# An attention stage whose engines follow one timetable, with a quarter of VectorE's subtractions given to GpSimd

## What is computed

```
Q, K, V = x1 projected by Wq, Wk, Wv (256 x 256), 16 heads of 16 channels, 512 positions, 8 batches
att = (Q K^T) / 4 + b;  att = att * m + (1 - m) * -1e30     # m: a mask value per key
y   = softmax(att) V
scores = y router_w;  the 2 best of 8 experts with normalized weights
out = x1 + sum over experts e of weight_e * down_e(silu(gate_e(y)) * up_e(y))
```

## Time and profile before

| | us |
|---|---|
| median of the runs | 3030.24 |
| profiled execution, its own time | 3030.47 |
| its span, first to last instruction | 3028.6 |
| TensorE busy | 2534.4 (84%) |
| VectorE busy | 2531.1 (84%) |
| ScalarE busy | 1214.7 (40%) |
| GpSimd busy | 1348.8 (45%) |

### The profile page before, as it was taken

The page is one execution under the profiler, slowest core; times in us unless marked ns, Lnnn a source line. Parts: engine busy times, 40 slices in busy tenths (PEclk is TensorE's granted clock), DMA queues, the critical chain, the costliest instruction groups (busy, mean ns, idle before and its releaser), DMA issues. The chain is left out here.

```text
span 3028.6 us, 112026 instructions
## 1 busy us (share of the span) xinstructions
PE 2534.4 (84%) x41104; PEld 1773.0 (59%) x41104; DVE 2531.1 (84%) x11914; ACT 1214.7 (40%) x4102; POOL 1348.8 (45%) x3951
## 2 busy tenths in 40 slices
PE   4478888888888888888888778888888876999999
PEld 4356666666666666666666546666666652444444
DVE  7989999999999999999998459999999976445544
ACT  3343333333333333333333348888888850000000
POOL 6846566656565656655655224434343344000000
PEclk6599999999999999999999889999999998999999
DMA  4100000000000000000000341111111110000000
GB/s 183 43 20 3 10 10 10 10 3 10 10 10 3 10 10 10 10 3 10 10 10 3 129 136 47 32 30 47 47 47 47 33 71 0 15 13 28 0 28 14
DMA packets 43893, 88.57 MB, mean 29 GB/s; under 512 B 7168, under 2 KB 23808, under 8 KB 41600
## 3 DMA queue, kind: packets, MB, share of 16 engines
q1 hardware_dynamic: 36336, 63.11, 6.6%
q10 hardware_dynamic: 4752, 10.49, 0.9%
q0 software_dynamic: 2304, 8.39, 0.9%
HBM read 65.18 MB, written 16.78 MB: 27 GB/s over the span
## 5 line engine op out<-in xcount | busy, mean ns | idle before, releaser
L228 PE MATMUL rest<-Tl,CW 128*128 128x56 f16 x16384 | 618.9, 190 | 313.5 <-DVE Tl L494 313.5
L228 PEld LDWEIGHTS rest<-Tl,CW 128*128 128x128 f16 x16384 | 503.3, 97 | 560.5 <-DVE Tl L494 556.6
L347 ACT ACTIVATE Tf<-X 128x32 f32<-128x32 f32 x768 | 176.0, 229 | 778.5 <-DVE X L538 778.5
L1082 ACT ACTIVATE Pr<-negL,nM 128x512 f32<-128x512 f32 x512 | 357.9, 729 | 16.8 <-DVE nM L1112 16.8
L1112 DVE CUSTOM_DVE_ANT_0 negL<-Lps,negC 128x512 f32<-128x512 f32 x512 | 339.6, 682 | 21.2 <-PE Lps L1020 18.0
L1030 PE MATMUL Tps<-idS,Pr 128*128 128x128 f32 x2048 | 282.9, 282 | 87.2 <-ACT Pr L1082 86.9
L1132 DVE TENSOR_TENSOR PT<-Tps,PT 128x512 f16<-128x512 f32 x512 | 348.2, 681 | 7.3 <-ACT PT L1089 2.5
L625 POOL TENSOR_TENSOR G<-X,Dr 128x32 f32<-128x32 f32 x768 | 205.9, 268 | 301.7 <-DVE X L499 274.2
L1089 ACT ACTIVATE PT<-Tps 128x512 f16<-128x512 f32 x512 | 292.3, 597 | 98.1 <-PE Tps L1030 98.0
L1030 PEld LDWEIGHTS Tps<-idS,Pr 128*128 128x128 f32 x2048 | 222.0, 142 | 177.5 <-ACT Pr L1082 148.3
L217 PE MATMUL main<-Th,CW 128*128 128x56 f16 x8224 | 264.1, 189 | 10.2 <-DVE CW L450 10.2
(11 more groups left out here) (133 smaller groups left out, 5147.1 us busy)
## 6 DMA issues: line engine op xcount, KB each, us to landing
stage<-w_up SPq DMA_DIRECT2D x8, 1024.0 KB, 4.8
qk<-qkp ACTq DMA_DIRECT2D x32, 256.0 KB, 2.4
QR<-qk SPq DMA_DIRECT2D x128, 64.0 KB, 2.2
KR<-qk SPq DMA_DIRECT2D x128, 64.0 KB, 2.4
wstage<-moe_up POOLq DMA_DIRECT2D x16, 512.0 KB, 5.4
W2m<-w_down SPq DMA_DIRECT2D x1, 4096.0 KB, 13.4
stage<-x_tb SPq DMA_DIRECT2D x16, 256.0 KB, 2.7
x<-stage SPq DMA_DIRECT2D x16, 256.0 KB, 2.1
```

The costliest lines, as they stand in the source:

```text
L228: last = pe.matmul(rest[:, m], CW[:, 0, k, m * P:(m + 1) * P], Tl[:, k:k + 1, :].to_broadcast([P, REP, B]), start=(m == 0 and k == 0), sto ...
L1082: act.activation(Pr[:, h % 2, qt, :], negL[:, qt, :], ACT.Exp, bias=nM[:, h % 4, qt:qt + 1], scale=-1.0).then_inc(s_exp, 1)
```

## The change

**Heads in one line.** The index `j` runs over all 128 heads, and every engine has a new order within a step. **Tile 3** (`KD` = 3, the last key tile) is no longer split by ScalarE and VectorE: ScalarE copies it in f32 to `last_f`, and GpSimd casts and subtracts it (`split_last`). **The products with V** are made in halves, queries 0 and 1 at the end of one step, 2 and 3 early in the next. **`negC` has two buffers**, so the mask terms of the next batch, their sum included, are made in head 12. The `halt` instructions behind most waits of this part are gone.

```diff
@@ GpSimd, heads
+            def split_last(b, h):
+                i = b * NH + h
+                pool.wait_ge(s_cp, i + 1 + AHEAD)
+                pool.tensor_copy(PT[:, h % 2, 0, KD, :], last_f[:, h % 2]).then_inc(s_ph, 1)
+                pool.wait_ge(s_ph, i + 1)
+                pool.tensor_tensor(PT[:, h % 2, 1, KD, :], last_f[:, h % 2], PT[:, h % 2, 0, KD, :],
+                                   ALU.subtract).then_inc(s_pl, 1)
+            def step(j):
+                if real(j - 2):
+                    split_last(*at(j - 2))
...
@@ TensorE, heads
-            def values(b, h):
+            def values(b, h, qts):
                 i = b * NH + h
-                pe.wait_ge(s_lo, DC * i + DC + AHEAD)
-                pe.wait_ge(s_norm, i - 1 + AHEAD)
+                if qts[0] == 0:
+                    pe.wait_ge(s_lo, KD * i + KD + AHEAD)
+                    pe.wait_ge(s_pl, i + 1 + AHEAD)
+                    pe.wait_ge(s_norm, i - 1 + AHEAD)
...
@@ ScalarE, heads
-                for qt, kcs in ((0, (0, 1)), (1, (2,)), (2, (3,)), (3, ())):
+                for qt, kcs in ((0, ()), (1, (0, 1, 2)), (2, (3,)), (3, ())):
```

In the experts the first gate and up products go ahead of the router products, and `route(g)` handles the 4 tiles of one group, once the first expert's hidden values are made:

```diff
-            route()
-            with dve.Fori(0, NG) as g:
+            for g in range(NG):
                 hidden(g, 0, 0)
                 hidden(g, 0, 1)
+                route(g)
                 dve.wait_ge(acc_in, (g + 1) * TT * 16)
-                dve.sem_inc(halt, 1)
```

More of the change, by code:

```diff
@@ L900, in _, with at, real @@
                     load_qk(sp, b + 1, half)
[L901 to L920, removed]
+                sp.wait_ge(negc_t, 3 * b + 6)
+                sp.dma_start(mrow[:], mask[b + 2].partition_broadcast(P)).then_inc(in_mask, 16)
+            for half in range(2):
+                sp.wait_ge(s_L, (B - 2) * 64 + 32 * (half + 1))
+                load_qk(sp, B - 1, half)
+        N = B * NH
+        def at(i):
+            return divmod(i, NH)
+        def real(i):
+            return 0 <= i < N
         @block.gpsimd
@@ L1001, in step @@
                     split_weights(b, (h - 5) // 4, (h - 5) % 4)
-                if h == 12:
+                if h == 12 and b + 1 < B:
                     mask_terms(b + 1)
-            pool.sem_inc(negc_ok, 1)
-            mask_terms(0)
-            all_heads(pool, step)
+            pool.sem_inc(negc_ok, 2)
+            pool.sem_inc(negc_t, 3)
+            for j in range(N + 3):
+                step(j)
         @block.tensor
@@ L1048, in values, with score, step @@
                                          start=False, stop=(kc == DC - 1), skip_group_check=True)
[L1049 to L1069, removed]
+                if qts[-1] == DC - 1:
+                    last.then_inc(s_pv, 1)
+            def score(i, qt):
+                if real(i):
+                    b, h = at(i)
+                    if h % (NH // 2) == 0 and qt == 0:
+                        pe.wait_ge(qk_in[h // (NH // 2)], b * QKI + QKI)
+                    scores(b, h, qt)
+            def step(j):
+                score(j, 1)
+                if real(j - 3):
+                    values(*at(j - 3), (2, 3))
+                score(j, 2)
+                for kc in (0, 1):
+                    if real(j - 1):
+                        transposes(*at(j - 1), kc)
+                score(j, 3)
+                for kc in (2, 3):
+                    if real(j - 1):
+                        transposes(*at(j - 1), kc)
+                score(j + 1, 0)
+                if real(j - 2):
+                    values(*at(j - 2), (0, 1))
+            score(0, 0)
+            for j in range(N + 3):
+                step(j)
         @block.scalar
@@ L1088, in transposed_high, with step @@
                 act.wait_ge(s_pv, i - 1 + AHEAD)
[L1089 to L1099 removed]
+                if kc < KD:
+                    act.activation(PT[:, h % 2, 0, kc, :], Tps[kc][:, :], ACT.Copy).then_inc(s_hi, 1)
+                else:
+                    act.wait_ge(s_pl, i - 1 + AHEAD)
+                    act.activation(last_f[:, h % 2], Tps[kc][:, :], ACT.Copy).then_inc(s_cp, 1)
+            def step(j):
+                for qt, kcs in ((0, ()), (1, (0, 1, 2)), (2, (3,)), (3, ())):
+                    if real(j):
+                        exps(*at(j), qt)
+                    for kc in kcs:
+                        if real(j - 1):
+                            transposed_high(*at(j - 1), kc)
+            for j in range(N + 1):
+                step(j)
         @block.vector
```

245 lines of the change are left out of this document (133 added, 112 removed).

## The result

The changed kernel takes 2976.67 us (median of four runs, 2975.05 to 2977.76) against 3029.05 (four runs, 3026.84 to 3032.59): a ratio of 0.9826, with a 95% interval of 0.9809 to 0.9843. Forecast were 2969 us and a range of 2943 to 3004. The profiled execution has a span of 2976.0 us, 52.6 less than before.

| stretch | before | after | change | forecast |
|---|---|---|---|---|
| start to the first minimum of attention | 1793.6 | 1797.7 | +4.1 | -1 |
| to the last low half of the output | 679.8 | 640.3 | -39.5 | -44 |
| experts, to the end of the span | 555.3 | 538.0 | -17.2 | -16 |

The account below looks back on a forecast made before the run. Attention was taken as bound by VectorE (5.11 us a head) and a loop through TensorE and ScalarE (5.24). Heads 71, GpSimd -26, drain -1, experts 16, projection 1 sum to 61 off 3030.47: 2969 us, range 2943 to 3004.

Parts of the forecast that it names:

- Two bounds at once: Attention head before: VectorE's instructions need 5.11 us, the loop transposes, ScalarE copies, exps 5.24; relieving one gains 0.13 or nothing.
- The new head, 4.67: Attention: a head takes 4.67 us instead of 5.24, between 4.59 and 4.80, gaining 71 us over 124 heads.
- VectorE's ring: Attention: VectorE's once-a-head cycle of seven steps, the wait for the reciprocal's result, and the scaling, 4.63 us.
- TensorE's ring: Attention: TensorE's once-a-head cycle of scores, transposes and products with V, without idle time, 4.59 us (4.54 to 4.64).
- The loop: Attention, new order: the dependency cycle through TensorE, ScalarE, GpSimd and VectorE comes to 4.62 us a head.
- the handshake: Attention: three minimums in a row with two score buffers; the third's tile needs 1.18 us against 1.21, fitting by 0.03.
- GpSimd, 26 us: Attention: TensorE waits where GpSimd is late with weights and mask terms, 26 us lost, between 12 and 36.
- The clock: Rival, chance 0.08: TensorE's 2 us waits at the masks bring its clock to 1.2 GHz, 21 us less gained, 2990.
- Start of attention, nothing: Start of attention: the first batch's mask terms and one DMA issue leave it, gaining nothing as TensorE waited for K anyway.
- Experts, 16: Experts: TensorE reaches the third expert's piece near 2524 us instead of 2542.33; 16 us gained, between 8 and 20.
- The rival that rings don't close: Attention rival, chance 0.15: many signals with small slack let a head settle at 4.9 to 5.0 us, about 3003.
- GpSimd as the bound: Attention rival, chance 0.05: GpSimd, held up by VectorE's instructions, needs 6.15 us a head, total 3130 us.

Follow-up runs that it names:

- experiments 1 and 2: 1: kernel before with only tile 3's split moved to GpSimd, 3052.33 us; 2: changed kernel with tile 3 split by ScalarE and VectorE again, 3020.6 us.
- experiment 7: Changed kernel with mask instructions spread over heads 12 to 15, reciprocal and scaling set apart, and the first expert weight load later: 2943.84 us.
- Experiment 4: Changed kernel with GpSimd's four mask instructions of a batch spread one each over heads 12 to 15: 2953.02 us.
- experiment 6: Changed kernel with the first load of expert weights held back until the first score tile: 2975.69 us.
- experiment 5: Changed kernel with VectorE's third minimum of a head put between the reciprocal and the scaling: 2977.16 us.

## Why the prediction came out as it did

- **Two bounds at once** (5.11 for VectorE, 5.24 for the loop): right, and shown by experiments 1 and 2. Tile 3 alone lost 22 us, the order with the experts gained 10, together they gained 52. Neither alone gains a thing in the heads. The kernel before shows VectorE's own bound too: just behind a batch's start, where it had waited for the mask terms and is behind, a head takes 5.10 us without a wait on VectorE.

```profile
1884.33 0.28 DVE L1126 TENSOR_TENSOR yn<-Ops,ri 128x128 f32<-128x128 f32 x1
...
1889.43 0.28 DVE L1126 TENSOR_TENSOR yn<-Ops,ri 128x128 f32<-128x128 f32 x1
```

- **The new head, 4.67**: measured 4.72. The mis-sized term is VectorE's ring, worked out as 4.23 + 0.21 + 0.19 = 4.63. What follows a reciprocal and needs its result starts 0.28 behind it, not 0.21, and the one behind the scaling 0.21 later, not 0.19. With these the ring is 4.72 to the last digit: 124 x 0.05 = 6 us too much was forecast. TensorE's ring was put too low as well, 4.59 (4.54 to 4.64): in experiment 7, where it never stands still, it is 4.68. That cost nothing here, as VectorE's was longer. The loop and the handshake (1.18 against 1.21) did close, since VectorE doesn't wait; how long the loop is by itself no run shows. The drain, from the last minimum to the last low half, came 0.3 us longer, where 1 was forecast.
- **GpSimd, 26 us**: measured 26.9, but that was luck: the sum was right and its parts wrong. The weights, for which half the high end stood (0.6 a step, twice a batch), cost nothing: with the extra semaphore instruction gone the gap between GpSimd's instructions is 0.08 (2001.59 + 0.61 to 2002.28), not 0.17, which was the case behind the low end, 12 us. The mask terms alone cost all of it, 12.4 us as waits (1.7 to 2.0 in each of seven places, against 1.7 to 2.4 forecast) and about 14.5 us through the clock.
- **The clock** stood as a rival with a chance of 0.08 and a price of 21 us on top. It happened, in six of seven places. Its mechanism was right, and it cost 14.5, less than its price. That the total was still near came from the weights' part, which fell away. Experiment 4 shows it.
- **Start of attention, nothing**: wrong, 3 us. The step that failed is "The mask terms of the first batch and one DMA issue leave the start of attention, where TensorE waited for K in any case: nothing." I didn't ask what GpSimd would issue earlier once they are gone. It was the load of the weights (experiment 6); by the other traces 2 to 3 us is its usual cost. The other 1 us of the +4.1 lies in front of it, where the last Q and K product ends 0.9 us later than before; the first one had started 1.9 us later (1713.81 against 1711.92), so the projection itself was about 1 us shorter, as forecast, but something ahead of it took it back. The traces of this same code differ there by up to 3.2 us from run to run (that product ends at 1772.6 in experiment 2 and at 1775.8 in experiment 4), so this is not settled.
- **Experts, 16**: 19.1 us at the third piece, of which 1.9 were given back by the end of the span, 17.2. Right, also in how: the third piece came 11.8 us behind the end of GpSimd's long instruction (2476.01), where 12 to 16 were expected, and alone the edit was worth 18.6.
- **The signs named in advance**: heads 4.72 apart and minimum and subtraction at 0.68 and 0.69, as said; the third piece 49.9 us behind attention, as said; TensorE's idle time ahead of the products is 12.4 us, at the low edge of 12 to 36, and only behind the masks, not behind the weights; VectorE idle under 3% holds away from the masks only, and is 6% over four batches.
- **The rival that rings don't close** had its mark at 4.9 us a head and never appeared. **GpSimd as the bound** neither: it needs 2.9 us of 4.72 in an ordinary head, and its casts and subtractions kept to 0.61 and 1.16 beside VectorE.

## What to carry to other kernels

When two bounds lie close together (here 5.11 and 5.24), work out what each edit gives alone: an edit that loses by itself can be the necessary half of a gain. An engine whose average is far from full still delays others if its extra work comes in one piece; the slack is that of one period, so cut such work to fit it (24 us here for moving three of four instructions). And once an engine is relieved at a stage's start, look at which of its DMAs moves forward, and what it then stands ahead of.

## What the runs showed of the hardware

- A wait of TensorE of only 1.7 to 2.2 us was enough to bring its clock to 1.2 GHz, in six of seven places in the changed kernel and in all seven of experiment 5, for 3.4 or 6.8 us at a time; each fall cost 1.5 to 3 us on top of the wait. In between, TensorE had hardly any idle time. Heads with 0.7 us of idle time each, as before, never brought it down. The third place was spared in the changed kernel and again in experiment 6, with a wait of 1.73 us, no shorter than the others; why is open.
- On VectorE, an instruction that needs the result of a small one right ahead of it starts 0.28 us behind it; one that doesn't, 0.09 behind.
- On GpSimd a small semaphore instruction between two others costs 0.09 us (gaps of 0.17 with it, 0.08 without).
- The issue of eight DMAs on SP's queue took 3.8 to 4.3 us instead of 3.7 while a 1 MB load ran ahead of them (five traces against six), and the last of K landed 2.2 to 3.4 us later, counted from the start of its issue.
